# A delta-rule stage whose products are put in another order within each step

## The reference, cut to what matters

```python
mixed_qkv = silu(causal_depthwise_conv(einsum('bsh,ch->bcs', x, Wqkv), conv_w))   # 4 taps
query, key, value = split(mixed_qkv)            # 16 key heads, each serves 2 value heads
q, k = l2norm(query) / sqrt(128), l2norm(key)
beta, g = sigmoid(b), -exp(A_log) * softplus(a + dt_bias)
for t in range(64):                             # per row of the batch and value head
    state = state * exp(g_t)
    delta = (v_t - state^T k_t) * beta_t
    state = state + k_t delta^T
    out_t = state^T q_t
out = rmsnorm(out) * norm_w * silu(x @ Wz)
y = einsum('bsv,hv->bsh', out, Wout)            # added to x
```

## Time and profile before

| | |
|---|---|
| time, median of 3 runs | 4804.81 us |
| the profiled execution's own time | 4818.4 us |
| its span | 4816.6 us |
| TensorE matmul busy | 4031.8 us (84%), 62044 instructions |
| TensorE weight load busy | 2628.2 us (55%), 62052 instructions |
| VectorE / ScalarE / GpSimd busy | 3118.6 (65%) / 2207.2 (46%) / 1508.8 us (31%) |
| mean granted TensorE clock of the core | 0.930 |
| the delta-rule stage | from about 2237 to 4161 us |
| in it, 2320.1 to 4099.7 us | TensorE matmul 1641.6 busy, VectorE 1230.9, ScalarE 1052.2, GpSimd 694.6 |

### The profile page before, as it was taken

The page is one execution under the profiler, slowest core; times in us unless marked ns, Lnnn a source line. Parts: engine busy times, 40 slices in busy tenths (PEclk is TensorE's granted clock), DMA queues, the critical chain, the costliest instruction groups (busy, mean ns, idle before and its releaser), DMA issues. The chain is left out here.

```text
span 4816.6 us, 143021 instructions
## 1 busy us (share of the span) xinstructions
PE 4031.8 (84%) x62044; PEld 2628.2 (55%) x62052; DVE 3118.6 (65%) x5769; ACT 2207.2 (46%) x4151; POOL 1508.8 (31%) x1605
## 2 busy tenths in 40 slices
PE   7527886677767887997899999999999999689999
PEld 6415654323325664444666666666666666455555
DVE  7897745788897886754666666676667766431111
ACT  3446533544444554323655555566655656221111
POOL 1001100298892220001434433333433333112222
PEclk9868997888989998999999999999999999789999
DMA  1000000233340001001000000000000000031111
GB/s 34 19 27 11 2 12 20 72 119 120 121 140 29 2 2 34 19 1 41 19 21 21 21 21 21 21 25 21 23 21 21 21 17 4 8 125 53 50 53 44
DMA packets 72967, 175.10 MB, mean 36 GB/s; under 512 B 14578, under 2 KB 27892, under 8 KB 69748
## 3 DMA queue, kind: packets, MB, share of 16 engines
q1 hardware_dynamic: 72340, 165.96, 10.9%
HBM read 163.04 MB, written 2.88 MB: 34 GB/s over the span
## 5 line engine op out<-in xcount | busy, mean ns | idle before, releaser
L1721 POOL TENSOR_TENSOR ssm_ub<-ssm_dtu,ssm_bcn 128x512 f32<-128x512 f32 x256 | 324.8, 1296 | 299.6 <-DMA ssm_bcn<-ssm_bct 297.2
L2539 POOL TENSOR_TENSOR dn_eb<-dn_ee,dn_cc 128x512 f32<-128x512 f32 x64 | 66.7, 1043 | 966.2 <-DVE dn_cc L2650 966.2
L3080 DVE TENSOR_TENSOR moe_hh<-moe_si,moe_pu 128x512 f32<-128x512 f32 x104 | 71.5, 688 | 450.4 <-PE moe_pu L2969 444.2
L2585 DVE SCALAR_TENSOR_TENSOR core_XN<-dn_bA,dn_w,core_XN 128x504 f32<-128x504 f32 (+2 forms) x384 | 280.8, 731 | 20.2 <-issue 1.3
L2209 PE MATMUL dn_pm<-dn_zz,dn_XB 32*32 32x32 f32 x16384 | 213.3, 195 | 90.4 <-issue 89.6
L1620 ACT ACTIVATE ssm_da<-core_XN,ssm_al 128x504 f32<-128x504 f32 x240 | 163.3, 683 | 253.3 <-DVE ssm_ph L1788 168.9
L3013 ACT ACTIVATE moe_si<-moe_pg 128x512 f32<-128x512 f32 x104 | 62.1, 597 | 466.1 <-PE moe_pg L2969 466.1
L3032 POOL TENSOR_TENSOR moe_hw<-moe_hh,moe_cb 128x512 f32<-128x512 f32 x100 | 126.5, 1265 | 444.9 <-DVE moe_hh L3080 392.0
L1608 PE MATMUL ssm_py<-ssm_hc,core_ident 128*128 128x512 f32 x352 | 201.9, 680 | 60.7 <-DVE ssm_yy L1773 30.4
L2185 PE MATMUL dn_bA<-core_XT,dn_w 128*128 128x512 f32 x512 | 244.6, 600 | 1.9 <-ACT dn_vv L2431 1.7
L2361 PE MATMUL dn_po<-dn_wo,dn_cT 128*128 128x256 f32 x1024 | 237.7, 386 | 2.8 <-issue 1.6
(11 more groups left out here) (500 smaller groups left out, 10360.7 us busy)
## 6 DMA issues: line engine op xcount, KB each, us to landing
ssm_bcn<-ssm_bct SPq DMA_DIRECT2D x128, 512.0 KB, 3.7
dn_cb<-dn_cum SPq DMA_DIRECT2D x32, 512.0 KB, 4.8
dn_w<-in_dn_w SPq DMA_DIRECT2D x32, 388.0 KB, 3.5
moe_cb<-moe_rows SPq DMA_DIRECT2D x64, 192.0 KB, 2.8
moe_w<-in_moe_w SPq DMA_DIRECT2D x26, 384.0 KB, 7.2
moe_cb<-moe_rows SPq DMA_DIRECT2D x64, 128.0 KB, 3.0
dn_wo<-in_dn_w SPq DMA_DIRECT2D x16, 256.0 KB, 2.7
moe_cb<-moe_rows SPq DMA_DIRECT2D x64, 64.0 KB, 2.6
```

Source lines behind the costliest of these rows:

```text
L1721: pool.tensor_tensor(ub[u % NUB][:, :], dtu[q % 2][:, c, :], bcn[i % NB][:, 0, :], ALU.mult).then_inc(ub_ready, 1)
L2585: last = dve.scalar_tensor_tensor(dst[:, :, n:S], src[:, :, 0:S - n], w[i // NCH % 2][:, at:at + 1], dst[:, :, n:S], ALU.mult, ALU.add)
```

## The change

`turn` and `out` are now those of i-4 (`ending`), and the pipeline runs one step longer. `first` goes to bank bD, where `gram` writes later, and ssq and its transpose to bC. `XB` has three buffers, `rb` four. The core of the diff:

```diff
-            for i in range(NSTEP + 3):
+            for i in range(NSTEP + 4):
...
-                    if q == 2 and 2 <= kh < NKH:
+                    if q == 3 and 2 <= kh < NKH:
                         load_wo(kh)
...
+                    if new:
+                        project(i, 1, bB)
+                        if i:
+                            take(pe, vv_done, 2)
+                        project(i, 2, bC)
...
+                    if ending:
+                        take(pe, cn_ready)
+                        for n in range(NS):
+                            mm = pe.transpose(po[:, n // 4, (n % 4) * P:(n % 4 + 1) * P], cn[:, n, :], g.ident[:, :])
+                        mm.then_inc(ct_ready, 1)
...
+                    if ending:
+                        take(pe, cT_ready)
...
+                    if new:
+                        project(i, 3, bA)
+                        take(pe, raw_free)
+                        take(pe, silu_ready, 2)
...
+                    if new:
+                        take(pe, sqr_ready)
+                        pe.transpose(bC[:, P:2 * P], sqr[:, :], g.ident[:, :]).then_inc(sst_ready, 1)
+                        gate(i, 0, bB)
+                    if old:
                         take(pe, y_added)
...
                         mm.then_inc(mp_ready, 1)
+                    if new:
+                        take(pe, tq_done)
+                        gate(i, 1, bC)
...
+                    if i + 1 < NSTEP:
+                        take(pe, pt_done)
+                        first(i + 1)
                     if old:
                         take(pe, mt_ready)
...
+                    if late:
+                        copy_z(even, -1.0)
+                        if old:
+                            take(act, mp_ready)
+                        diagonal(i - 2)
...
+                        if i:
+                            conv(i, 3, bA)
...
                         dve.tensor_tensor(pairs(PT[i % 3]), kq[:, :, 1, :].unsqueeze(2).broadcast_to([P, TPC, 2, S]),
-                                          pairs(kp_), ALU.mult)
+                                          pairs(kp_), ALU.mult).then_inc(pt_done, 1)
```

More of the change, by code:

```diff
@@ L2031, in l3_attn @@
         wo = [s.sb(f"wo{k}", [P, 2, D]) for k in range(2)]
-        XB = [s.sb(f"XB{k}", [P, 2, NS * HB]) for k in range(2)]
+        XB = [s.sb(f"XB{k}", [P, 2, NS * HB]) for k in range(3)]
         XF = s.sb("XF", [P, NS, S])
@@ new lines, in step @@
+                    if i == 0:
+                        running()
+                    if ending:
[3 more added lines that the diff above has]
+                        mm.then_inc(ct_ready, 1)
+                    if mid:
+                        take(pe, zz_ready)
+                    if late:
+                        level_z(i - 2, 4)
@@ new lines, in step @@
+                    if mid:
+                        level_x(i - 1, 1, odd)
+                    if ending:
+                        take(pe, cT_ready)
+                        if e % NCH == 0:
+                            take(pe, wo_ready)
+                        for j in range(TPC):
+                            for h in range(2):
+                                mm = pe.matmul(po[:, j // 2, (j % 2) * D:(j % 2 + 1) * D], cT[:, h * TPC + j, :],
+                                               wo[e // NCH % 2][:, h, :], start=h == 0, stop=h == 1)
+                        mm.then_inc(y_ready, 1)
@@ L2291, in step @@
                         mm.then_inc(o_ready, 1)
[L2292 to L2334, removed]
                     if new:
@@ L2338, in step @@
                         values(0, bA)
[L2339 to L2351, removed]
                         take(pe, silu_ready)
-                        take(pe, zs_done)
+                        take(pe, zs_done, 2)
                         values(1, bC)
[L2355 to L2369, removed]
                 schedule(step)
@@ L2457, in step @@
                         tap(i, 1, bB)
+                        tap(i, 2, bC)
+                    if i == 0:
+                        running()
+                    if ending:
+                        take(act, ct_ready)
+                        act.activation(cT[:, :, :], heads(po[:, :, :]), ACT.Copy).then_inc(cT_ready, 1)
+                    if late:
+                        copy_z(even)
+                    if new:
+                        act.preload_act_table_set("silu_and_others")
+                        silu(0)
+                        silu(1)
+                        act.drain()
+                        act.activation(sqq[:, :], cv[:, 1, :], ACT.Square).then_inc(sq_ready, 1)
+                    if mid:
+                        copy_z(odd)
+                    if new:
+                        silu(2)
+                        tap(i, 3, bA)
+                        take(act, ssq_ready)
+                        act.activation(sqr[:, :], bC[:, 0:P], ACT.Copy).then_inc(sqr_ready, 1)
+                    if late:
+                        copy_z(even, -1.0)
+                        if old:
+                            take(act, mp_ready)
+                        diagonal(i - 2)
+                    if new:
+                        gate(i, 0, bB)
+                        gate(i, 1, bC)
+                        if i % NCH == NCH - 1:
+                            act.sem_inc(w_free, 1)
+                        silu_turned(3)
+                    if mid:
+                        copy_z(odd)
+                    if late:
+                        corner()
                     if old:
```

196 lines of the change are left out of this document (96 added, 100 removed).

## The result

The changed kernel took 4841.45 us (median of 4 runs, 4839.05 to 4862.62), the one before 4804.19 us beside it: ratio 1.0092, 95% interval 1.006 to 1.0124. It is slower by 37 us, where I had forecast 4788 and put the upper end of the range at 4840. The profiled execution took 4839.05 us with a span of 4837.2.

The account below looks back on a forecast made before the run. TensorE was taken as near its bound, the rest late instruction blocks, clock falls and a VectorE wait. New step 28.2 + 0.45 + 0.1 = 28.75 us against 29.17, -26 us, +9 at the ends: 4788 us, range 4737 to about 4840.

Parts of the forecast that it names:

- The loop, 28.2 us: Chain from M through conv A, `PT`, `first`, O, values and C to the next M: floor of the step, 28.2 us.
- The waits that come: New TensorE waits in each step: 1.58 us before `first` for `PT`, 0.64 us before C for the value copies.
- The waits at rounds under 45 us: Sign to look for: TensorE's waits with no releaser before round products fall from 92.4 to under 45 us.
- Late blocks, 0.45 us a step: Instruction blocks of 256 still arriving late at pairs of rounds: 0.45 us a step, bounds 0.1 and 1.0.
- The clock, 0.1 us a step: Clock falls behind the new wait before `first`: 0.1 us a step, bounds 0 and 0.8.
- The ends, +9 us: Longer end of the stage, from the last `first`, 94 us before and 103 after: +9 us, bounds 0 and +15.
- The sum: Step of 28.2 + 0.45 + 0.1 = 28.75 us against 29.17; with the ends, -17 us.
- the third: Rival: idle before `first` makes the clock fall; at one fall in two steps, 29.5 us a step, 4834 us; 20%.
- The fourth: Rival: waits at round products go with rounds as such, not late blocks; 29.7 us a step, 4846 us; 10%.
- The first: Rival: handovers overlap more than walked and TensorE stays the bound; 26.0 + 0.45 us a step, 4648 us; 5%.
- the second: Rival: the loop takes it all, `cT` late by 0.3 us or `conv A` waiting; step 29.0, about 4804 us; 20%.

Follow-up runs that it names:

- e10_even_fill: Changed kernel with three throwaway 128x256 products in the wait before `first` and 56 small instructions ahead of values A, 1536 instructions a step: 4782.27 us, ratio 0.9955.
- e5_even: Changed kernel with 17 throwaway 32x32 products ahead of values A, 1536 instructions a step, and 50 instructions more in step 3: 4806.82 us, ratio 1.0004.
- e2_fill: Changed kernel with three throwaway 128x256 products in TensorE's wait before `first`: 4831.7 us, ratio 1.006 to the kernel before.
- e6_uneven: Same padding of the changed kernel as e5_even, but with 92 instead of 50 more instructions in step 3: 5030.62 us, ratio 1.0475.
- e1_pt_first: Changed kernel with `PT` ahead of conv A on VectorE: 4737.83 us, ratio 0.9867 to the kernel before.
- e8_pt_tap: On top of e1_pt_first, ScalarE makes the two value copies before `tap first`: 4737.37 us, ratio 0.9862 to the kernel before.

## Why the prediction was wrong

Point by point, in the prediction's own steps.

- **The loop, 28.2 us: right.** Measured 28.32. From M to `first` 5.29 (5.23 forecast), `first` 1.92 (1.82), O to C 5.81 (6.01), C to the next M 15.3 (15.16). e10_even_fill shows it bare.
- **The waits that come: right.** Before `first` mostly 1.3 to 1.5 us (forecast 1.58), before C 0.54 (0.64), none before `out`, none before values A. I was a little high on both because TensorE's own work is 28.32 - 1.34 - 0.54 = 26.4 us and not 26.0; inside the loop the waits took that up.
- **The waits at rounds under 45 us: right,** 34.4. The clock rose above 0.97, as I had said, but only to 0.98, with 21 falls where my 0.1 us a step allows for about four.
- **Late blocks, 0.45 us a step: too small.** The 60 steps are 1772.2 - 60 x 28.32 = 73 us longer than undisturbed ones; 35 us of it are falls (below), which leaves 38 us, 0.63 a step. e5_even agrees: without late blocks its 60 steps are 41.4 us shorter, 5 of them by three falls fewer. It is within the bounds of 0.1 and 1.0. My reading that a block can't follow the one before in less than 3.7 to 3.9 us was made from one stall and is too long: packets of the instruction queue ended as little as 3.28 us apart in the trace of before and 3.24 in that of after.
- **The clock, 0.1 us a step: the step that failed.** 21 falls x 1.65 us = 35 us, 0.58 a step. The 15 falls behind the wait before `first` make 0.41 of it, the 6 behind late blocks the rest. I had set the price of a fall right, 1.7 us. What I had wrong is how often a fall comes behind the wait before `first`. I took the earlier trace rows, a fall behind 2.02 us, and 0.84 us without one as the bounds, and set the new 1.58 us close to the harmless end. The trace of before has more to say than these two rows: of its idle times of 1.6 to 1.8 us 7 of 11 have a fall behind them, and between 1.3 and 1.6 us it has only three, without one. So it gave little ground for 0.1 us, one fall in 17 steps, at a wait of 1.58 us. In the changed kernel a wait of 1.32 to 1.48 us behind a pair had a fall in 13 of 53 steps, in e5_even such a wait had one in 18 of 60. e2_fill, which fills the wait at the same loop, has 3 falls in place of 21.
- **The ends, +9 us: the number is right by luck.** I had put all of it behind the last `first`, 94 us before and 103 after. Counted so, 94.0 became 109.2 us, +15: the four chains behind M(60) take 86 us and not 80. The +9.1 above is another count, around the 60 steps of `Mt`: 15.1 more at the start, which I had not looked at, and 6.0 less at the end.
- **The sum.** 28.32 + 0.63 + 0.58 = 29.5 us against 28.75. The steps are 0.12 + 0.18 + 0.48 = 0.8 us longer than forecast, 47 us in 60 steps, most of them by the clock, the late blocks' 0.18 the next; from -17 to +30 us in the stage, measured +32.

Of the rivals, the third was nearest: it gave 4834 us for a fall in every second step. There were 21 falls in 60 steps, about one in three and not one in two, and late blocks made up the rest. The fourth, that the waits go with rounds as such, is excluded by e5_even and e6_uneven, which have the same rounds. The first is excluded by the wait in each step. Of the second, no wait before `out` came. The Trainium skill, "Runtime: NRT & Kernel Launch", section "Instruction fetch mechanics", has fetching in 16 KiB blocks mostly hidden by dispatch. The measurement decides: blocks of 256 agree (345 packets for 87483 instructions), hidden they are not, 34.4 us after and 92.4 before.

The step measured, 29.54 us, lies within the 29.6 from which the range's upper end of 4840 was worked out. The result is 1.5 us above that end because the medians lie 5 us further apart than the stage accounts for; of these 5 us the profiles show nothing.

The direction hung on one sum: 1.48 us more of loop (I had 1.4) against 2.3 us of disturbance, of which I thought 1.8 us would go and 1.1 went. e1_pt_first shows that the change needn't have paid for it: in the old order conv A came ahead of `BT` and `PT`; the change put it between them, and as `first` now waits for `PT`, its 2.5 us of VectorE became part of TensorE's loop.

## What to carry to other kernels

When a new order makes an instruction of the bounding engine wait for another engine, walk that engine's list backwards from the signal and ask what could stand behind it instead: here one VectorE instruction was worth 104 us. Price each idle time twice, once for itself and once for the clock behind it, and take the chance of a fall from all idle times of like length in the trace, not from one. And where an engine stalls with no releaser between bursts of small instructions, count instructions: a few dozen more or less can move a block's boundary into or out of the burst, so compare two orders only with their boundaries held in place; here a difference of 2% could come from the boundaries alone.

## What the hardware showed that I had not expected

- **Late blocks.** A stalled TensorE goes on about 1.4 us after the last packet of the instruction queue has ended (1.2 to 1.65 us), and in the stage no two packets ended less than 3.15 us apart, in any of the twelve traces. 256 instructions of 32x32 products run in 1.25 us. The largest effect of position was 224 us of 4807, by 42 instructions (e5_even, e6_uneven).
- **Padding as a gain.** 68 instructions of throwaway products a step made the old kernel 91 us faster (ratio 0.9824, 0.9793 to 0.9854) and, with `PT` ahead, the new one 117 us faster than before.
- **A fall behind 1.3 us.** Idle times of 1.32 to 1.48 us behind round products had a fall of the clock to 1.2 GHz behind them in 13 of 53 steps, at 1.65 us a fall. In e5_even, where every step has the same instructions and the same wait, 18 of 60 fell: what decides between equal steps stays open.
- **A wait can be useful.** Taking away the wait of about 0.5 us before C (e8_pt_tap) brought 9.5 us more of late blocks and five more falls, and no time.
